# Expert groups in units 4 to 14 instead of 3 to 14, and the diagonal selects of units 1 to 3 split anew between GpSimd and VectorE

## Chip, cores and metric

The kernel runs on one core of a Trainium2 chip. The metric is device microseconds of one execution. A core has five engines with an instruction stream each: TensorE (PE), VectorE (DVE), ScalarE (ACT), GpSimd (POOL) and SyncE (SP, which here only issues transfers). Each stream runs strictly in its own order; semaphores tie the streams together.

## What is computed

A transformer layer without mask padding: x is 4 x 1024 tokens of 128 numbers, all float32. The layer norm xn goes into two branches, whose results are added to x.

```python
def _L0_attn_ref(x, w_qkv, w_proj, b_proj):          # 16 heads of 8, causal
    q, k, v = jnp.split(x @ w_qkv, 3, axis=-1)
    ...
    wei = jnp.einsum('bhqd,bhkd->bhqk', q, k) * scale
    wei = jnp.where(causal, wei, -jnp.inf)
    wei = jax.nn.softmax(wei, axis=-1)
    out = jnp.einsum('bhqk,bhkd->bhqd', wei, v)
    ...
    return out @ w_proj + b_proj

def _L0_ffn_ref(x, Wg, W1, b1, W2, b2):               # 8 experts of 512, the best 2 of each token
    logits = xt @ Wg.T
    topk_logits, topk_idx = jax.lax.top_k(logits, TOP_K)
    w = jax.nn.softmax(topk_logits, axis=-1)
    ...
    h = jax.nn.gelu(jnp.einsum('th,ehi->tei', xt, W1) + b1, approximate=False)
    o = jnp.einsum('tei,eih->teh', h, W2) + b2
    y = jnp.einsum('te,teh->th', gates, o)
x = x + _L0_attn_ref(xn, ...) + _L0_ffn_ref(xn, ...)
```

## The kernel before

**Units and steps.** The attention is cut into 16 units (4 sequences x 4 groups of 4 heads). A unit has ten steps, `SUB`: steps 0 to 2 take the triangle of the first 512 queries (1, 2 and 1 blocks of 128 x 128 on the diagonal), steps 3 to 6 the full square, steps 7 to 9 the triangle of the last 512 queries. "(n, s)" below is unit n, step s. In a step PE makes transposed scores for two pairs of heads ("scores", L919), ACT turns them into `probs` with the exponential (L804), the part above the diagonal is set to zero in the steps of `DIAG`, and PE multiplies with v ("values", L936). The values of step s stand in PE's stream within step s + 1. `probs` has two buffers by step, so the exponentials of step s wait for the values of step s - 2.

**Maxima.** The exact row maxima are found ahead: "max" parts (L899 on PE, L1134 and L1136 on DVE), 36 a unit, are taken from one stream that runs some 27 ahead of the unit. `counts(n)` says how many each step takes.

**The triangles.** Two ways do the same: `SELS`, an affine select on GpSimd (L720), and `CLEARS`, a scalar_tensor_tensor on DVE (L1146) that multiplies with a 0/1 triangle. `scatters_in(n, s)` chooses: DVE where it is true. Before, that is all diagonal steps of units 1 and 2 and steps 0 to 2 of unit 3. PE's values wait for whichever it is.

**Experts.** DVE sorts the tokens by expert while unit 0 runs (the "route" parts). GpSimd then scatters the 32 tiles of normed rows twice (two experts a token) to `xs` in HBM with 64 indirect DMAs (L712), one part "scatter" each, spread over 20 steps from (0, 9) to (2, 8), three or four at the end of each step. A scatter waits for the second last before it to have landed (`UNDER_WAY` = 2). The 39 blocks of 256 sorted rows are done in groups, one group a unit, `FFN_UNIT` = units 3 to 14, three or four blocks each: sizes 3, 3, 3, 4, three times over. SP loads a group's rows ("load_rows", L603), w1 ("load_up", L615), w2 and biases ("load_down", L625 to L630). PE transposes the rows ("rows_in", L977), ACT and DVE split them into a high part (L834) and a low part (L1073), then come "hidden" (12 products a block on PE, L853 to L855, four Gelus on ACT, L816) and "down" (two a block, L997, added to the bias on DVE, L1184), and GpSimd sends the rows back with an indirect DMA ("send", L735).

**The general group** (units 4 to 14): its rows are loaded in step 6 of the unit before and transposed in steps 8 and 9, each before the values of that step's part. All its hidden blocks stand at the start of the unit, ahead of step 0, with three maxima behind each (`BESIDE_M`). The downs stand in steps 1 to 8 or 2 to 7.

**Group 0** (unit 3) is an exception: its rows need all scatters. So they are loaded in (3, 3), transposed in (3, 5) and (3, 6), its hidden blocks stand at the end of (3, 6) and its downs in (3, 7) and (3, 8). SP waits for all scatters at "load_rows" and at the first "reload" (L594, x read again for the residual), both in (3, 3).

**The fill.** `fill` adds "warm" products without use (L949) to a step whose PE work is under `aim(n, s)` columns: 2900 in units of `FFN_UNIT`, 4000 in the others, 3300 in the last.

Of the kernel before, what the change touches and what calls it, by code (L numbers as in the profile page):

```python
# [22 lines left out]
UNITS = B * G4  # L23
# [41 lines left out]
SECOND = 3  # L65
# [6 lines left out]
HALF_M = HG * 3  # L72
EARLY_M = 18

FFN_UNIT = list(range(3, UNITS - 1))
GROUP_OF = {u: f for f, u in enumerate(FFN_UNIT)}
NGRP = len(FFN_UNIT)
FIRST = [NBLK * f // NGRP for f in range(NGRP + 1)]
# [1 line left out]

NORM_TILES = [range(0, 4), range(4, 8)] + [range(TPB * b, TPB * b + TPB) for b in range(1, B)]
PIECES = 13
CLEAR_FROM, CLEAR_UNTIL = (1, 0), (3, SECOND)
SCATTER_FROM, SCATTER_STEPS = 9, 20
UNDER_WAY = 2
VECTOR_NORMS = 3
BESIDE_M = 3
# [3 lines left out]
def scatters_in(n, s):  # L91


    return CLEAR_FROM <= (n, s) < CLEAR_UNTIL


def blocks_of(f):

    return range(FIRST[f], FIRST[f + 1])
# [33 lines left out]
def with_negations(group):  # L133


    return list(group) + [("negate", x[1], int(x[2] == NM - 1)) for x in group if x[2] in (HALF_M - 1, NM - 1)]
# [40 lines left out]
def row_phase(n, s, maxima):  # L177


    low, high = [x for x in maxima if x[2] % HG < 2], [x for x in maxima if x[2] % HG >= 2]  # L180
    first = [(low, 1), (high, 0)] if len(low) >= len(high) else [(high, 0), (low, 1)]
    parts = []
    for beside, half in first:
        parts += beside[:1] + [("scores", n, s, half)] + beside[1:]
    return parts


def counts(n):


    if n in GROUP_OF and GROUP_OF[n] > 0:
        rest = NM - BESIDE_M * len(blocks_of(GROUP_OF[n]))
        return [rest * (i + 1) // NS - rest * i // NS for i in range(NS)]
    first = [9, 9] if n == 0 else [5, 4]
    rest = 0 if n == UNITS - 1 else 27 - (BESIDE_M * len(blocks_of(0)) if n == FFN_UNIT[0] else 0)
    return first + [rest * (i + 1) // 8 - rest * i // 8 for i in range(8)]


def unit_parts(n, stream):

    parts, f, nf = [], GROUP_OF.get(n), GROUP_OF.get(n + 1)
    late_rows = []

    def take(count):
        group = with_negations([next(stream) for _ in range(count)])
        late_rows.extend(("rows",) + x[1:] for x in group if x[0] == "negate")
        return group

    def late_values():
        if n > 0:  # L210
            parts.extend([("values", n - 1, NS - 1), ("evacuate", n - 1, 1)])

    if n >= 1 and n + 2 < UNITS:
        parts.append(("relay", n + 2))
    if f:
        for b in blocks_of(f):
            parts.append(("hidden", f, b))
            if b - FIRST[f] == 1:
                late_values()
            parts.extend(take(BESIDE_M))  # L220
        if f + 1 < NGRP:
            parts.append(("load_up", f + 1))
    subs = [(b, u) for b in blocks_of(f) for u in range(BK // P)] if f is not None else []
    step_of = [7, 7, 7, 8, 8, 8] if f == 0 else list(range(2, 8)) if len(subs) == 6 else list(range(1, 9))
    for s in range(NS):
        due, late_rows[:] = list(late_rows), []
        group = take(counts(n)[s])
        parts.append(("step", n, s))
        only = [x for x in group if x[0] == "max"]
        parts.extend(row_phase(n, s, only[:4]))  # L230
        parts.extend(x for x in group if x not in only[:4])
        if s == 0 and not f:
            late_values()
        if nf and s in (8, 9):
            parts.append(("rows_in", nf, s - 8))
        if s > 0:
            parts.append(("values", n, s - 1))
        parts.extend(due)
        parts.extend(BESIDE.get((n, s), []))
        if s == 1 and n > 0:  # L240
            parts.append(("turn", n - 1, 1))
        parts.extend(("send", f) + x for x, at in zip(subs, step_of) if at == s - 1)
        parts.extend(("down", f) + x for x, at in zip(subs, step_of) if at == s)
        if s == SECOND:
            parts.append(("evacuate", n, 0))
        if s == 3 and n % G4 == 0 and n > 0:
            parts.append(("columns", n // G4 - 1, 1))
        if s == 5:
            parts.append(("turn", n, 0))
        if s in (4, 6) and (n == 6 or (n % G4 == 0 and n > G4)):  # L250
            parts.append(("project", 0 if n == 6 else n // G4 - 1, s // 2 - 2))
        if s in (2, 3, 4, 5) and n % G4 == 1 and n // G4 + 1 < B:
            parts.append(("qk", n // G4 + 1, s % 2, s // 2 - 1))
        if s == 7 and n % G4 == G4 - 1:
            parts.append(("columns", n // G4, 0))
        if s == NS - 1 and n == UNITS - 1:
            parts.append(("project", B - 1, 0))
        if (n, s) in ((2, 3), (2, 7)):
            parts.append(("load_up", 0) if s == 3 else ("load_down", 0))
        if f == 0 and s == 3:  # L260
            parts.append(("load_rows", 0))
        if f == 0 and s in (3, 5, 7, 8):
            parts.append(("reload", (3, 5, 7, 8).index(s)))
        if f == 0 and s in (5, 6):
            parts.append(("rows_in", 0, s - 5))
        if f == 0 and s == 6:
            for b in blocks_of(0):
                parts.append(("hidden", 0, b))
                parts.extend(take(BESIDE_M))
            parts.append(("load_up", 1))  # L270
        if s == (9 if f == 0 else 8) and f is not None and f + 1 < NGRP:
            parts.append(("load_down", f + 1))
        if nf and s == 6:
            parts.append(("load_rows", nf))
        step = NS * n + s - SCATTER_FROM
        if 0 <= step < SCATTER_STEPS:
            parts.extend([("scatter", 0, 0)] * (TOPK * NT * (step + 1) // SCATTER_STEPS - TOPK * NT * step // SCATTER_STEPS))
        if n == UNITS - 1 and s in (0, 2):
            parts.extend(("fetch_back", b) for b in range(B) if (b > 0) == (s > 0))
        if n == UNITS - 1 and s in (2, 4, 6, 8):  # L280
            b = (2, 4, 6, 8).index(s)
            parts.append(("combine", b))
            if b < B - 1:
                parts.append(("store", b, 0))
    parts.extend(late_rows)
    return parts
# [70 lines left out]
EVAC = {x: i for i, x in enumerate(x for x in SCHED if x[0] == "evacuate")}  # L357

SELS = {x: i for i, x in enumerate(x for x in SCHED if x[0] == "scores" and x[2] in DIAG and not scatters_in(*x[1:3]))}
CLEARS = {x: i for i, x in enumerate(x for x in SCHED if x[0] == "scores" and x[2] in DIAG and scatters_in(*x[1:3]))}  # L360
TURNS = {x: i for i, x in enumerate(x for x in SCHED if x[0] == "turn")}
# [878 lines left out]
```

How the kernel before makes its waits and increments, by code:

```python
def wait(eng, sem, value):  # L392
    if value > 0:
        eng.wait_ge(sem, value)
# [136 lines left out]
        @block.sync  # L532
# [9 lines left out]
            sp.dma_start(b2s, b2).then_inc(b_loaded, 16)  # L542
            sp.dma_start(bps, b_proj.partition_broadcast(E)).then_inc(b_loaded, 16)
            experts = {}
            for part in SCHED:
                what = part[0]
                if what == "relay":
                    n = part[1]
                    i, rows = n % 3, slice(32 * (n % G4), 32 * (n % G4) + 32)
                    if n < 3:
                        sp.wait_ge(zeroed, 7)
                    else:
                        sp.wait_ge(sc_ready, both(PAIRI, n - 3, NS - 1))
                    if n % G4 == 0:
                        sp.wait_ge(aux_d, D_AFTER["qk", n // G4, 1, 1])
                    for r in range(3):
                        sp.dma_start(kT[i][r:P:4, :].bitcast(F32), (kqh, kql, kqh)[r][rows, 0, :].bitcast(F32)) \
                            .then_inc(relayed[i], 16)
# [4 lines left out]
                    if n >= 3:  # L564
                        sp.dma_start(qT[i][3:P:4, :].bitcast(F32), mid(zero[0:32, :], T // P)).then_inc(relayed[i], 16)
                elif what == "bias_out":
                    sp.wait_ge(smallT_done, 1)
                    sp.dma_start(b1_scr.rearrange("p e c -> p (e c)"), b1T).then_inc(b_stored, 16)
                    sp.wait_ge(b_summed, 1)
                    sp.dma_start(b2_scr, b2s).then_inc(b_stored, 16)
                elif what == "fetch":
```

## Time and profile before

| | us |
|---|---|
| median of 3 runs | 746.47 |
| the runs | 744.14, 746.47, 948.12 |
| the profiled execution | 744.73 |
| its span, first to last instruction | 742.8 |

Engines busy in the span: PE 659.0 us (89%), DVE 529.3 (71%), ACT 441.5 (59%), POOL 265.0 (36%). The mean granted clock of TensorE is 0.90 of full speed; it moves between 0.5 (1.2 GHz) and 1.0 (2.4 GHz). All times below are microseconds from the start of the span.

The windows further down run between two starts of PE's work. Those of rows 7 go from values product to values product: 163.2 (2, 0), 175.6 (2, 3), 191.6 (2, 8), 199.6 (3, 0), 213.2 (3, 3), 268.4 (4, 0), 277.2 (4, 3), 117.5 (1, 0), 154.6 (1, 8); the last one is a stretch of low clock. Those of rows 8 go from a unit's first hidden product to the next unit's; 255.78 is unit 4's.

### The profile page before, as it was taken

The page shows a single profiled execution, that of the slowest core. Times are in us where ns is not written, and L with a number is a line of the kernel's source. Part 1 is how long each engine was busy: PE and PEld are TensorE (multiplying, and loading weights), DVE is VectorE, ACT ScalarE, POOL GpSimd, SP SyncE. Part 2 cuts the span into 40 slices and gives each one's busy share as a digit, 9 for nine tenths or more (in the row PEclk, how much of TensorE's full clock was granted, in tenths as well). Part 3 has the DMA queues.
Part 4 walks back from the last instruction along what each step waited for, and adds up shares of the span by engine and source line. Part 5 has one row for each costly group of instructions (what it writes and reads, how often), then busy time and mean ns, then how long its engine had stood idle before and what let it go on. Part 6 is the DMA issues. An engine that isn't in the chain of part 4 may idle for free.

```text
span 742.8 us, 14540 instructions
## 1 busy us (share of the span) xinstructions
PE 659.0 (89%) x4867; PEld 385.9 (52%) x4867; DVE 529.3 (71%) x1805; ACT 441.5 (59%) x656; POOL 265.0 (36%) x423
## 2 busy tenths in 40 slices
PE   6899678888866999989999999899999999999986
PEld 5674334344424655545665555546565655555533
DVE  5758887697933576777677676777677776778666
ACT  5223454546434676768576776767576766667654
POOL 5813155655450423231333333231333232333411
PEclk9655796789866999999999999998999999999989
DMA  6651963134514735435251525335252616240075
GB/s 159 199 113 21 238 178 102 47 86 138 126 44 130 221 123 125 138 100 161 80 137 44 154 85 131 130 109 152 82 161 68 172 35 155 94 115 12 26 184 160
DMA packets 99289, 87.93 MB, mean 118 GB/s; under 512 B 13296, under 2 KB 86704, under 8 KB 99216
## 3 DMA queue, kind: packets, MB, share of 16 engines
q1 hardware_dynamic: 94320, 76.69, 38.6%
q0 software_dynamic: 4544, 9.35, 3.7%
q10 hardware_dynamic: 352, 0.97, 0.6%
q8 instruction: 39, 0.64, 0.4%
q14 instruction: 34, 0.28, 0.1%
HBM read 49.79 MB, written 20.80 MB: 95 GB/s over the span
## 4 chain that ended last, share of the span: by engine, by line
PE 63%; DVE 18%; ACT 9%; issue 5%; DMA 3%; ACTq 0%; POOL 0%; SPq 0%; DVEq 0%; POOLq 0%
PE ov L936 17%; PE aux L899 13%; PE aux L997 10%; DVE junk L1136 5%; ACT probs L804 3%; DVE maxes L1134 3%; PE sc L853 3%; PE aux L949 3%; PE aux L954 2%; PE sc L919 2%; PE sc L854 2%; PE sc L855 2%; DVE xrow L1197 2%; ACT hid L816 1%; ACT L804 1%
## 5 line engine op out<-in xcount | busy, mean ns | idle before, releaser
L804 ACT ACTIVATE probs<-sc 128x1024 f32<-128x1024 f32 (+1 forms) x320 | 286.6, 941 | 171.3 <-PE sc L919 156.5
L1136 DVE CUSTOM_DVE_ANT_0 junk<-aux,cst 128x128 bf16<-128x128 f32 (+3 forms) x512 | 220.5, 486 | 33.2 <-PE aux L899 30.1
L899 PE MATMUL aux<-kT,qT 32*128 32x512 f32 (+3 forms) x768 | 200.4, 446 | 34.5 <-DVE maxes L1136 8.1
L1134 DVE TENSOR_REDUCE maxes<-aux 128x1 f32<-128x512 f32 x256 | 163.2, 683 | 38.3 <-PE aux L899 33.5
L720 POOL TENSOR_SCALAR_AFFINE_SELECT probs<-probs 128x256 f32<-128x256 f32 x216 | 85.3, 408 | 275.2 <-ACT probs L804 270.3
L936 PE MATMUL ov<-probs,v 128*32 128x512 f32 (+3 forms) x1536 | 173.5, 542 | 0.7 <-POOL probs L720 0.6
L899 PEld LDWEIGHTS aux<-kT,qT 32*128 32x128 f32 x768 | 90.3, 197 | 123.5 <-DVE maxes L1136 29.9
L919 PE MATMUL sc<-qT,kT 32*128 32x512 f32 (+3 forms) x768 | 142.7, 427 | 5.5 <-DMA qT<-mT 3.2
L735 POOL DMA_INDIRECT ys<-ysb,back x78 | 75.5, 968 | 101.9 <-DVE ysb L1184 55.4
L997 PEld LDWEIGHTS aux<-w2all,hid 128*128 128x128 f32 x624 | 77.6, 196 | 38.2 <-DVE maxes L1134 22.6
L997 PE MATMUL aux<-w2all,hid 128*128 128x128 f32 x624 | 89.3, 288 | 0.3 <-DVE kql L1073 0.3
L712 POOL DMA_INDIRECT xs<-xrow,wall x64 | 62.4, 974 | 50.6 <-DMA xs<-xrow,wall 26.1
L816 ACT ACTIVATE hid<-sc,bias 128x256 f32<-128x256 f32 x156 | 61.2, 476 | 27.4 <-PE sc L855 26.4
L919 PEld LDWEIGHTS sc<-qT,kT 32*128 32x128 f32 x768 | 68.8, 195 | 13.7 <-ACT probs L804 7.5
L936 PEld LDWEIGHTS ov<-probs,v 128*32 128x32 f32 x1536 | 34.9, 113 | 53.1 <-issue 45.3
L1184 DVE TENSOR_TENSOR ysb<-aux,bias 128x128 f32<-128x128 f32 x78 | 22.7, 291 | 48.2 <-PE aux L997 47.3
L949 PE MATMUL aux<-wh 128*128 128x384 f32 x174 | 48.8, 400 | 7.9 <-DVE maxes L1136 4.6
L853 PE MATMUL sc<-xsh,w1b 128*128 128x256 f32 x156 | 48.2, 309 | 0.0
L949 PEld LDWEIGHTS aux<-wh 128*128 128x128 f32 x174 | 32.8, 215 | 24.6 <-DVE maxes L1136 13.0
L854 PE MATMUL sc<-xsl,w1b 128*128 128x256 f32 x156 | 44.1, 283 | 0.0
L855 PE MATMUL sc<-xsh,w1b 128*128 128x256 f32 x156 | 44.0, 282 | 0.0
L1136 DVE DVE_READ_ACCUMULATOR2_ANT maxes<- 128x1 f32 x512 | 42.3, 83 | 0.0
(121 smaller groups left out, 605.3 us busy)
## 6 DMA issues: line engine op xcount, KB each, us to landing
w1b<-w_scr SPq DMA_DIRECT2D x39, 512.0 KB, 4.8
w2all<-in_L_ffn_W SPq DMA_DIRECT2D x39, 256.0 KB
xs<-ysb SPq DMA_DIRECT2D x13, 387.0 KB, 8.1
kT<-kqh SPq DMA_DIRECT2D x32, 128.0 KB
w_scr<-w1b SPq DMA_DIRECT2D x8, 512.0 KB
qT<-kqh SPq DMA_DIRECT2D x30, 128.0 KB
xrow<-in_L_attn_x SPq DMA_DIRECT2D x7, 512.0 KB, 5.8
xsin<-xs SPq DMA_DIRECT2D x9, 387.0 KB
```

Source lines behind the costliest of these rows:

```text
L720: last_ = nc.gpsimd.affine_select(out=block_, in_=block_, compare_op=ALU.is_ge, fill=0.0, base=0, pattern=[[0, 2], [1, P]], channel_multip ...
L735: nc.gpsimd.indirect_dma_start(out=ys[:, :], out_offset=bass.IndirectOffsetOnAxis(ap=back[:, f % 2, i:i + 1], axis=0), in_=ysb[:, i, :], i ...
L804: nc.scalar.activation(probs[:, s % 2, 2 * half:2 * half + 2, 0:cols], pair(part)[:, :, 0:cols], ACT.Exp).then_inc(sc_done, 1)
L816: last_ = nc.scalar.activation(hid[:, i, ch, :], pair(part)[:, ch // 2, BK * (ch % 2):BK * (ch % 2) + BK], ACT.Gelu, bias=bias[i][:, ch:ch ...
L853: nc.tensor.matmul(out_, wh_, mh, start=True, stop=False)
L899: last_ = nc.tensor.matmul(bank(part)[:, at:at + cols], qT[n % 3][rows, P * i:P * i + P], kT[n % 3][rows, k0:k0 + cols], start=True, stop= ...
L919: last_ = nc.tensor.matmul(pair(part)[:, h % 2, at:at + cols], kT[n % 3][rows, P * j:P * j + P], qT[n % 3][rows, q:q + cols], start=True, ...
L936: last_ = nc.tensor.matmul(ov[32 * h:32 * h + 32, W - cols:W], v[:, vat:vat + 32], probs[:, s % 2, h, at:at + cols], start=(j == 0), stop= ...
L949: nc.tensor.matmul(bank(unit)[:, 0:FILL], src[:, 0:P], src[:, 0:FILL], start=True, stop=True)
L997: last_ = nc.tensor.matmul(bank(part)[:, 0:C], hid[:, i, ch, P * u:P * u + P], w2b[i][:, ch, :], start=(ch == 0), stop=(ch == CH - 1))
L1134: last_ = nc.vector.reduce_max(dst, src, axis=AX.X)
L1136: last_ = nc.vector.tensor_tensor_reduce(out=junk[:, AUXI[part] % 3, at:at + cols], in0=src, in1=cmask[:, W - cols:W], scale=1.0, scalar=L ...
```

## The change

- `FFN_UNIT` becomes units 4 to 14, so eleven groups share the 39 blocks: 3, 4, 3, 4, 3, 4, 3, 4, 3, 4, 4. Group 0 (still three blocks) stands in unit 4 in the general form: hidden blocks ahead of step 0, downs in steps 2 to 7.
- What is special about group 0 stays only in its loads: w1 in (3, 3), w2 and biases in (3, 7), where before it was (2, 3) and (2, 7); rows in (3, 8), transposed both at the end of (3, 9), behind the values there. The reloads of x move from unit 3 to unit 4.
- Unit 3 has no expert work. Its aim is then 4000 columns a step, and its maxima are spread as in unit 2.
- `scatters_in` is true only for steps from 3 on, and up to the end of unit 3: the steps 7 to 9 of units 1 to 3 are cleared on DVE, the steps 0 to 2 of units 1 to 3 are selected on GpSimd. There they stand in GpSimd's stream between the scatters, each at the place of its step.
- The scatters keep their places.

```diff
--- before.py
+++ after.py
@@ -72,7 +72,7 @@
 HALF_M = HG * 3
 EARLY_M = 18
 
-FFN_UNIT = list(range(3, UNITS - 1))
+FFN_UNIT = list(range(4, UNITS - 1))
 GROUP_OF = {u: f for f, u in enumerate(FFN_UNIT)}
 NGRP = len(FFN_UNIT)
 FIRST = [NBLK * f // NGRP for f in range(NGRP + 1)]
@@ -80,7 +80,7 @@
 
 NORM_TILES = [range(0, 4), range(4, 8)] + [range(TPB * b, TPB * b + TPB) for b in range(1, B)]
 PIECES = 13
-CLEAR_FROM, CLEAR_UNTIL = (1, 0), (3, SECOND)
+CLEAR_FROM, CLEAR_UNTIL = (1, 0), (4, 0)
 SCATTER_FROM, SCATTER_STEPS = 9, 20
 UNDER_WAY = 2
 VECTOR_NORMS = 3
@@ -91,7 +91,7 @@
 def scatters_in(n, s):
 
 
-    return CLEAR_FROM <= (n, s) < CLEAR_UNTIL
+    return CLEAR_FROM <= (n, s) < CLEAR_UNTIL and s >= SECOND
 
 
 def blocks_of(f):
@@ -188,11 +188,11 @@
 def counts(n):
 
 
-    if n in GROUP_OF and GROUP_OF[n] > 0:
+    if n in GROUP_OF:
         rest = NM - BESIDE_M * len(blocks_of(GROUP_OF[n]))
         return [rest * (i + 1) // NS - rest * i // NS for i in range(NS)]
     first = [9, 9] if n == 0 else [5, 4]
-    rest = 0 if n == UNITS - 1 else 27 - (BESIDE_M * len(blocks_of(0)) if n == FFN_UNIT[0] else 0)
+    rest = 0 if n == UNITS - 1 else 27
     return first + [rest * (i + 1) // 8 - rest * i // 8 for i in range(8)]
 
 
@@ -212,7 +212,7 @@
 
     if n >= 1 and n + 2 < UNITS:
         parts.append(("relay", n + 2))
-    if f:
+    if f is not None:
         for b in blocks_of(f):
             parts.append(("hidden", f, b))
             if b - FIRST[f] == 1:
@@ -221,7 +221,7 @@
         if f + 1 < NGRP:
             parts.append(("load_up", f + 1))
     subs = [(b, u) for b in blocks_of(f) for u in range(BK // P)] if f is not None else []
-    step_of = [7, 7, 7, 8, 8, 8] if f == 0 else list(range(2, 8)) if len(subs) == 6 else list(range(1, 9))
+    step_of = list(range(2, 8)) if len(subs) == 6 else list(range(1, 9))
     for s in range(NS):
         due, late_rows[:] = list(late_rows), []
         group = take(counts(n)[s])
@@ -229,7 +229,7 @@
         only = [x for x in group if x[0] == "max"]
         parts.extend(row_phase(n, s, only[:4]))
         parts.extend(x for x in group if x not in only[:4])
-        if s == 0 and not f:
+        if s == 0 and f is None:
             late_values()
         if nf and s in (8, 9):
             parts.append(("rows_in", nf, s - 8))
@@ -255,23 +255,18 @@
             parts.append(("columns", n // G4, 0))
         if s == NS - 1 and n == UNITS - 1:
             parts.append(("project", B - 1, 0))
-        if (n, s) in ((2, 3), (2, 7)):
+        if nf == 0 and s in (3, 7):
             parts.append(("load_up", 0) if s == 3 else ("load_down", 0))
-        if f == 0 and s == 3:
+        if nf == 0 and s == 8:
             parts.append(("load_rows", 0))
         if f == 0 and s in (3, 5, 7, 8):
             parts.append(("reload", (3, 5, 7, 8).index(s)))
-        if f == 0 and s in (5, 6):
-            parts.append(("rows_in", 0, s - 5))
-        if f == 0 and s == 6:
-            for b in blocks_of(0):
-                parts.append(("hidden", 0, b))
-                parts.extend(take(BESIDE_M))
-            parts.append(("load_up", 1))
-        if s == (9 if f == 0 else 8) and f is not None and f + 1 < NGRP:
+        if s == 8 and f is not None and f + 1 < NGRP:
             parts.append(("load_down", f + 1))
         if nf and s == 6:
             parts.append(("load_rows", nf))
+        if nf == 0 and s == 9:
+            parts.extend(("rows_in", 0, i) for i in range(2))
         step = NS * n + s - SCATTER_FROM
         if 0 <= step < SCATTER_STEPS:
             parts.extend([("scatter", 0, 0)] * (TOPK * NT * (step + 1) // SCATTER_STEPS - TOPK * NT * step // SCATTER_STEPS))
```

## Rows read from the trace of the kernel before

**Rows 1.** Page, part 4: the chain that ended last, by engine.
```profile
PE 63%; DVE 18%; ACT 9%; issue 5%; DMA 3%; ACTq 0%; POOL 0%; SPq 0%; DVEq 0%; POOLq 0%
```

**Rows 2.** Timeline of PE (start us, us; in brackets the idle time before, and its releaser).
```profile
229.71 1.08 PE L977 MATMUL aux<-cst,xsin 128*128 128x128 f32 x4 [12.27 <-DMA xsin<-xs]
```

**Rows 3.** Timeline of GpSimd from 117 to 224: eight of the 64 scatters.
```profile
117.13 0.96 POOL L712 DMA_INDIRECT xs<-xrow,wall  x1 [0.30 <-issue]
...
169.50 0.96 POOL L712 DMA_INDIRECT xs<-xrow,wall  x1 [0.81 <-issue]
...
177.73 0.95 POOL L712 DMA_INDIRECT xs<-xrow,wall  x1 [2.59 <-DMA xs<-xrow,wall]
180.22 0.96 POOL L712 DMA_INDIRECT xs<-xrow,wall  x1 [1.53 <-DMA xs<-xrow,wall]
...
187.63 0.96 POOL L712 DMA_INDIRECT xs<-xrow,wall  x1 [1.92 <-DMA xs<-xrow,wall]
189.69 0.96 POOL L712 DMA_INDIRECT xs<-xrow,wall  x1 [1.10 <-DMA xs<-xrow,wall]
193.44 0.96 POOL L712 DMA_INDIRECT xs<-xrow,wall  x1 [2.79 <-DMA xs<-xrow,wall]
...
223.87 0.95 POOL L712 DMA_INDIRECT xs<-xrow,wall  x1 [0.78 <-DMA xs<-xrow,wall]
```

**Rows 4.** Timeline of PE: the first values products of (2, 2) and (3, 0).
```profile
172.48 0.64 PE L936 MATMUL ov<-probs,v 128*32 128x256 f32 x8
...
199.65 1.94 PE L936 MATMUL ov<-probs,v 128*32 128x512 f32 x8
```

**Rows 5.** Groups by line and form: busy us, mean ns; then idle before.
```profile
L720 POOL TENSOR_SCALAR_AFFINE_SELECT probs<-probs 128x256 f32<-128x256 f32 x216 | 85.3, 408 | 275.2 <-ACT probs L804 270.3 <-DVE maxes L1134 1.2 <-issue 0.3
...
L1146 DVE SCALAR_TENSOR_TENSOR probs<-probs,cst 128x256 f32<-128x256 f32 x40 | 16.1, 422 | 2.8 <-ACT probs L804 1.7 <-issue 1.0
...
L1073 DVE TENSOR_TENSOR xsl<-aux,xsh 128x512 fp32r<-128x512 f32 x15 | 10.4, 691 | 22.5 <-ACT xsh L834 22.5
...
L834 ACT CAST xsh<-aux 128x512 fp32r<-128x512 f32 x15 | 8.9, 593 | 13.6 <-PE aux L977 13.2
```

**Rows 6.** Timeline of SP's queue: w1 and w2 of group 0, its rows.
```profile
171.63 2.75 SPq L615 DMA_DIRECT2D w1b<-w_scr  x3
...
183.43 0.45 SPq L625 DMA_DIRECT2D w2all<-in_L_ffn_W  x1
...
226.21 0.39 SPq L603 DMA_DIRECT2D xsin<-xs  x1
```

**Rows 7.** Windows: length, busy PE PEld DVE ACT POOL, clock, DMA share, GB/s.
```profile
163.20:175.60 12.40, 11.21 (x82) 5.94 (x84) 9.85 (x43) 5.23 (x9) 6.96 (x8) 0.83 0.35 104
175.60:191.60 16.00, 13.98 (x103) 5.90 (x102) 13.73 (x39) 10.13 (x13) 6.94 (x7) 1.00 0.53 146
199.60:213.20 13.60, 12.47 (x65) 5.72 (x64) 7.48 (x32) 4.63 (x8) 8.17 (x9) 0.50 0.14 46
268.40:277.20 8.80, 8.30 (x85) 4.78 (x80) 5.87 (x25) 5.94 (x9) 3.80 (x8) 1.00 0.06 18
117.50:154.60 37.10, 32.51 (x181) 15.05 (x180) 26.63 (x86) 17.66 (x24) 22.79 (x24) 0.74 0.14 46
...
222.00:235.70 13.70, 5.99 (x29) 3.80 (x30) 2.49 (x10) 3.74 (x5) 2.10 (x3) 0.50 0.45 120
```

**Rows 8.** Windows from first hidden product to the next unit's: units 4, 10 to 13.
```profile
255.78:294.26 38.48, 36.20 (x305) 21.20 (x301) 28.68 (x99) 28.26 (x43) 15.57 (x28) 1.00 0.48 132
...
502.69:545.49 42.80, 41.36 (x329) 26.17 (x325) 29.59 (x101) 28.73 (x45) 12.66 (x23) 0.92 0.37 108
545.49:582.99 37.50, 35.74 (x306) 21.01 (x302) 28.28 (x99) 27.51 (x42) 13.66 (x26) 1.00 0.45 123
582.99:623.37 40.38, 37.62 (x322) 22.81 (x318) 29.52 (x101) 27.59 (x42) 12.25 (x23) 1.00 0.40 110
623.37:662.18 38.81, 36.98 (x304) 21.30 (x300) 28.38 (x99) 27.13 (x41) 12.25 (x23) 0.96 0.46 131
```

## The prediction

> **What bounds the kernel now.** I read the page first: the chain that ended last runs through PE for 63% of the span, DVE 18%, ACT 9%, GpSimd (POOL) 0% [rows 1]. So a stretch costs what PE has to do in it, and GpSimd's work costs nothing. The longest idle times of PE show the exception: once it waits 12.27 us, up to 229.71, for the load of the expert rows [rows 2]. GpSimd's and SP's timelines give the chain behind it: the last of 64 scatters starts on GpSimd at 223.87, SP issues the load of group 0's rows at 226.21, PE goes on 3.5 us later [rows 3, 6]. The transposes that wait stand in unit 3, step 5, and need every scatter; the written order ends the scatters in step 8 of unit 2, whose values start at 191.6 [rows 7]. They run 32 us behind it. The reason is that only two may be under way: a pair is issued 0.3 us apart, 0.96 each, then GpSimd waits 0.8 for a landing [rows 3], which makes 3.0 us a pair at best and more, up to 2.8 us a gap, where SP's transfers run.
>
> **Now GpSimd's order matters.** Before, units 1 and 2 ask nothing of GpSimd but scatters; DVE clears the triangles. After, the selects of steps 0 to 2 stand in GpSimd's queue behind the scatters of the steps before: three before (1,0) (unit, step), 35 before (2,0), 38 before (2,1), 41 before (2,2), and all 64 before (3,0). They are late by what is queued ahead of them. Behind a select waits the values product of its step, and behind that all of PE's stream.
>
> **What the selects cost.** One costs 408 ns on GpSimd, the clear on DVE 422 ns [rows 5]. Steps 0 to 2 have eight (1+2+1 blocks, two halves), so 24 move to GpSimd, and 8 (unit 3, steps 7 to 9) go to DVE. DVE gains 16 x 0.42 = 6.8 us net. I price that at nothing: where it falls PE will wait for GpSimd, or it works at half clock with DVE idle beside it, as in unit 3 before (PE busy 12.5 of 13.6 us, DVE 7.5 [rows 7]). If that cover were gone it would be worth the whole 6.8.
>
> The Trainium skill, page GPSIMD Engine Reference, § 4.1, speaks against the move: elementwise work belongs on VectorE, GpSimd being about twice as slow with two inputs and about equal with one. The two rows above have equal durations, the select having one input tensor; with twice the price the sum below would be about 7 us higher (an estimate).
>
> **Unit 1.** The fourth scatter starts at 117.13 after 0.30 idle, so the third ends at 116.83 [rows 3]; the two selects of (1,0) then end near 117.7, and the values product before started at 117.5 [rows 7]. The next two steps shift PE by 0.5 to 1 us and the scatters by about 1.2, since part of the 3.3 us of selects lies in the waits for a landing. No more.
>
> **Unit 2.** The 35th scatter started at 169.50 [rows 3]; with that shift it ends near 171.7. Its select follows, and values (2,0) start near 172.7 instead of 163.2 [rows 7]. Three scatters (two at 1.3, one at 1.9 with its wait) and four selects later it is (2,1) at about 178.4, then (2,2) at 183.5, before 172.48 [rows 4]. PE is 11 us late. It needs no select until (3,0): before, (2,2) to (3,0) took 199.65 - 172.48 = 27.2 us [rows 4], so it arrives at 210.7, some us later if its clock has fallen in the waits.
>
> **The last scatter.** Before it ended at 224.8 [rows 3]. Added: 1.2 (unit 1) and 2.0 (unit 2: 3.3 us of selects less what lies in landings). Removed: group 0's w1 and w2 loads, issued at 171.63 and 183.43 [rows 6], leave unit 2 for unit 3. Near them the gaps were 2.59 and 1.53, then 1.92 and 1.10, where an ordinary pair has 0.8 + 0.4 [rows 3]; that gives back 2.9 + 1.8. The relay of unit 5 that runs near 193 stays, and with it a gap of 2.79 and another like it. Sum: 224.8 + 3.2 - 4.7 = 223.3. Bounds: 219.4 if the relay's excess of 2 x 2 us goes as well, 231.4 if nothing is given back and all 16 selects count in full. Two selects on top: values (3,0) start at 224.2 instead of 199.65. PE waits up to 13 us there. The old wait of 12.3 us has moved, it is not gone.
>
> **Unit 3 from there.** No expert work, but filled up to 4000 columns a step and with the same maxima as unit 2, so unit 2 is the model. Its steps 0 to 3 took 12.4 us, at a mean clock of 0.83; unit 3's own took 13.6 at 0.50, unit 4's 8.8 at 1.00. After the wait the clock will be at its low level for a while, as it was from 222.0 to 235.7 [rows 7]. I take 12.4, bounds 8.8 and 13.6: (3,3) at 236.6. Steps 3 to 8 of unit 2 took 16.0 [rows 7]: (3,8) at 252.6, and its product takes 1.0. Now comes what other groups don't have: group 0's rows are loaded in step 8 and transposed in step 9, directly before the first hidden product. SP issues nine transfers (w2 and biases) ahead of that load; in unit 2 they began 8 us before (2,8). Alone, the load took under 3.5 us from issue [rows 2, 6]. I take 1 us of waiting (0 to 3). The load's own wait for the scatters is long over by step 8. Then four transposes (1.08 at the low clock [rows 2], I take 0.8), the cast 0.6 and the subtraction 0.7 [rows 5] are in sequence: 2.1. First hidden product of unit 4: 253.6 + 1.0 + 2.1 = 256.7, before 255.8 [rows 8]: +0.9 us. The four reloads of x go with group 0 into unit 4; the first reader is the projection in unit 6, so they cost nothing.
>
> **Units 4 to 15.** At that point the kernel before has group 0's three blocks behind it, the kernel after has not. Eleven groups follow in both, with 36 blocks before and 39 after. From first hidden product to first hidden product it took 42.8 us with four blocks (unit 10) and 37.5, 40.4 and 38.8 with three (units 11, 12, 13; 12 also projects) [rows 8]. PE is busy 41.4 and 37.0 of it in units 10 and 13: the block is PE work, and no cover hides it. I take unit 13, which like 10 has neither projection nor columns: 4.0 us a block, bounds 2.4 (against 12) and 5.3 (against 11). Three blocks: +12.0 us (7.2 to 15.9). What a group costs beside its blocks comes eleven times in both. The transfers of a fourth block are hidden: the DMA share in unit 10 is 0.37 [rows 8].
>
> **Sum.** 0.9 + 12.0 = +12.9 us on a span of 742.8: 755.7. The profiled execution took 744.7 in all, so 757.6. The median of the three runs, 746.5, is 1.8 above it; 757.6 is 1.5% above the median.
>
> **The rivals.**
> - *The queue holds PE, and the clock stays low behind it: slower by over 2%.* Place: unit 3, steps 0 to 8. Unit 1 took 37.1 us for them at a mean clock of 0.74 and with its qk products, unit 2 took 12.4 + 16.0 = 28.4 [rows 7]. If unit 3 costs as unit 1, +8.7: 766. It decides from +3.8 on, which is 761.4. For it: in unit 3 before the clock was low with PE busy. Against it: after the old wait it was back 6 us after PE went on [rows 2, 7]. Chance 0.18. A dearer block (5.3), or a scatter stream without relief, leads over the same line (761.5 and more): 0.18 together.
> - *The queue doesn't hold PE.* If GpSimd came to (3,0) by 210.7, all falls by 13.5: 744, no change. It would need 1.1 us a scatter from (2,2) on, below the 0.96 + 0.30 of two issues in a row [rows 3]. Chance 0.05.
> - *DVE was the bound in units 1 to 3.* Its 6.8 us count in full, with the low ends for block and steps: 757.6 - 6.8 - 4.8 - 3.6 = 742. DVE is busy 13.7 of 16.0 us in the second half of unit 2 [rows 7], but there nothing is taken from it. Chance 0.06. Below 731.5 comes only this together with the one above: 0.05.
> - *The forecast,* 746 to 761: 0.48.
>
> About 2% is what a measurement of this kernel can tell from no change, so faster means under 731.5 and slower over 761.4. Chances: faster 0.05, within 2% 0.48 + 0.05 + 0.06 = 0.59, slower 0.36. The low ends together (3.9 + 3.6 + 1.0 + 4.8) give 744.3, the high ends (8.1 + 1.2 + 2.0 + 3.9) 772.8; eight in ten lie in 746 to 769.
>
> **What would show each step.** Right: PE idle in front of values (2,0) and again some 10 us in front of (3,0), each wait ended by a GpSimd select; the last scatter at 219 to 227; no 12 us wait for the rows; first hidden product of unit 4 within 250 to 262; 499 us from there to the end instead of 487. Wrong: values (3,0) before 215; four blocks in a cycle under 41 us; scatters at 1.5 us each all through unit 2; the clock low through most of unit 3.

## The result, and the profile after

The changed kernel takes 758.5 us (median of four runs, 758.0 to 762.1). Beside it the kernel before took 745.3, a median over four runs with the 948.12 among them, which the ratios leave out like every other run in the chip's slower state. The ratio is 1.0191, 95% interval 1.0145 to 1.0238: clearly slower, but the 2% that was set to separate "no change" from "slower" lies inside the interval. The profiled execution took 758.3, its span is 756.2, against 755.7 forecast. The line numbers of the functions are five smaller than before (L931 is the values product that was L936).

The page's chain that ended last, by engine, to set beside [rows 1]:

```profile
PE 57%; DVE 16%; issue 12%; ACT 6%; DMA 5%; SPq 2%; POOL 1%; ACTq 0%; POOLq 0%; DVEq 0%
```

GpSimd itself is still nearly absent. But the page's split of this chain by line now has `DMA xs<-xrow,wall`, the landings of the scatters, with 3%. "issue" (time for which the profile shows no cause) went from 5% to 12%. In the list of waits (engine and line, releaser: us in total, times, the longest) one line has grown. Before it stood at 0.6 us, once:

```profile
PE ov L931 <- POOL probs L715: 27.4, 6, 11.0
```

PE's timeline (start us, us; idle before and its releaser) shows the two long ones, at values (2,0) and (3,0). Three of the other four are 1.83 us at (1,0), 2.09 at (1,1) and 1.53 at (2,1).

```profile
162.92 0.50 PE L894 MATMUL aux<-kT,qT 32*128 32x512 f32 x1
174.44 1.08 PE L931 MATMUL ov<-probs,v 128*32 128x512 f32 x4 [11.02 <-POOL probs L715]
...
213.42 0.79 PE L894 MATMUL aux<-kT,qT 32*128 32x512 f32 x1
224.64 1.88 PE L931 MATMUL ov<-probs,v 128*32 128x512 f32 x5 [10.43 <-POOL probs L715]
```

GpSimd's timeline at the same places shows why. The exponentials of (2,0) ended at 160.8 and those of (3,0) at 211.0; the selects came only when the 35th and the 64th scatter had been issued, nearly 13 us later, and both scatters had waited for landings:

```profile
172.56 0.96 POOL L707 DMA_INDIRECT xs<-xrow,wall  x1 [0.81 <-DMA xs<-xrow,wall]
173.53 0.77 POOL L715 TENSOR_SCALAR_AFFINE_SELECT probs<-probs 128x256 f32<-128x256 f32 x2
...
222.75 0.96 POOL L707 DMA_INDIRECT xs<-xrow,wall  x1 [0.81 <-DMA xs<-xrow,wall]
223.73 2.19 POOL L715 TENSOR_SCALAR_AFFINE_SELECT probs<-probs 128x256 f32<-128x256 f32 x6
```

The last row holds six selects in a stretch without a gap: two of (3,0) and four of (3,1) had been ready. The wait of [rows 2] is gone: group 0's rows now hold PE for 0.38 us, and the sequence of transposes, cast and subtraction for another 1.07:

```profile
252.99 1.94 PE L931 MATMUL ov<-probs,v 128*32 128x384 f32 x16
255.30 1.51 PE L972 MATMUL aux<-cst,xsin 128*128 128x128 f32 x6 [0.38 <-DMA xsin<-xs]
257.88 0.55 PE L848 MATMUL sc<-xsh,w1b 128*128 128x256 f32 x1 [1.07 <-DVE xsl L1068]
```

SP's queue, to set beside [rows 6]: the loads of w1 and w2 of group 0 are past the last scatter, the rows' load comes 5.8 us behind the first w2.

```profile
232.69 2.62 SPq L610 DMA_DIRECT2D w1b<-w_scr  x3
...
244.45 0.45 SPq L620 DMA_DIRECT2D w2all<-in_L_ffn_W  x1
...
250.20 0.39 SPq L598 DMA_DIRECT2D xsin<-xs  x1
```

Windows with the columns of [rows 7]: unit 3 from (3,0) to (3,3) and on to (3,8), then everything from unit 4's first hidden product to the end:

```profile
224.60:236.60 12.00, 10.98 (x81) 5.82 (x83) 6.09 (x29) 4.66 (x8) 2.13 (x6) 0.84 0.23 67
236.60:253.00 16.40, 14.07 (x102) 5.84 (x102) 14.13 (x39) 10.67 (x14) 0.00 (x0) 0.98 0.39 118
257.90:756.20 498.30, 467.11 (x3763) 282.84 (x3763) 354.71 (x1203) 334.18 (x501) 152.73 (x280) 0.97 0.43 119
```

The kernel before, from its first hidden product of unit 4 on, had three blocks less in the same eleven groups:

```profile
255.78:742.80 487.02, 452.31 (x3677) 268.54 (x3673) 351.22 (x1197) 329.66 (x490) 150.23 (x279) 0.97 0.41 114
```

So the 13.4 us of span split into +2.1 up to that product (257.9 against 255.8) and +11.3 behind it. The stretch before (3,0) is no fixed length either: three more profiles below (36 blocks, and rows early twice) are of kernels with the same instructions up to there. In the four of them PE reached the wait between 214.2 and 216.3 and left it between 223.8 and 225.2; the wait was 10.4, 9.7, 8.6 and 8.0 us. What PE loses before it, the wait gives back.

### The profile page after: what moved, and what is told of

Same layout as the page of the kernel before. It is cut to its first block, busy times and chain, and to the rows that moved or that the text cites. A ratio compares the mean times of both kernels' runs of the same rounds, so it can differ in the third digit from the quotient of the medians.

```text
span 756.2 us, 14558 instructions
## 1 busy us (share of the span) xinstructions
PE 660.9 (87%) x4884; PEld 390.1 (52%) x4884; DVE 524.9 (69%) x1787; ACT 438.8 (58%) x652; POOL 270.1 (36%) x438
## 4 chain that ended last, share of the span: by engine, by line
PE 57%; DVE 16%; issue 12%; ACT 6%; DMA 5%; SPq 2%; POOL 1%; ACTq 0%; POOLq 0%; DVEq 0%
PE ov L931 14%; PE aux L894 12%; PE aux L992 10%; DVE junk L1131 6%; PE sc L848 3%; ACT probs L799 3%; PE aux L944 3%; DMA xs<-xrow,wall 3%; PE aux L949 2%; PE sc L849 2%; PE sc L850 2%; PE sc L914 2%; DVE xrow L1192 2%; DVE maxes L1129 2%; PE aux L972 1%
## 5 line engine op out<-in xcount | busy, mean ns | idle before, releaser
L1131 DVE CUSTOM_DVE_ANT_0 junk<-aux,cst 128x512 bf16<-128x512 f32 (+3 forms) x512 | 219.6, 487 | 33.7 <-PE aux L894 28.5
L931 PE MATMUL ov<-probs,v 128*32 128x512 f32 (+3 forms) x1536 | 172.1, 538 | 27.7 <-POOL probs L715 27.4
L715 POOL TENSOR_SCALAR_AFFINE_SELECT probs<-probs 128x256 f32<-128x256 f32 x232 | 91.3, 408 | 280.1 <-ACT probs L799 274.6
L914 PE MATMUL sc<-qT,kT 32*128 32x512 f32 (+3 forms) x768 | 140.0, 423 | 5.6 <-DMA qT<-mT 3.3
L931 PEld LDWEIGHTS ov<-probs,v 128*32 128x32 f32 x1536 | 35.2, 113 | 80.9 <-issue 68.6
L944 PE MATMUL aux<-wh 128*128 128x384 f32 x191 | 52.3, 395 | 8.9 <-DVE maxes L1131 6.2
L944 PEld LDWEIGHTS aux<-wh 128*128 128x128 f32 x191 | 35.4, 212 | 26.4 <-DVE maxes L1131 15.3
```

The source lines that it names most:

```text
L715: last_ = nc.gpsimd.affine_select(out=block_, in_=block_, compare_op=ALU.is_ge, fill=0.0, base=0, pattern=[[0, 2], [1, P]], channel_multip ...
L914: last_ = nc.tensor.matmul(pair(part)[:, h % 2, at:at + cols], kT[n % 3][rows, P * j:P * j + P], qT[n % 3][rows, q:q + cols], start=True, ...
L931: last_ = nc.tensor.matmul(ov[32 * h:32 * h + 32, W - cols:W], v[:, vat:vat + 32], probs[:, s % 2, h, at:at + cols], start=(j == 0), stop= ...
L944: nc.tensor.matmul(bank(unit)[:, 0:FILL], src[:, 0:P], src[:, 0:FILL], start=True, stop=True)
L1131: last_ = nc.vector.tensor_tensor_reduce(out=junk[:, AUXI[part] % 3, at:at + cols], in0=src, in1=cmask[:, W - cols:W], scale=1.0, scalar=L ...
```

## The experiments

The theory: PE pays for selects that stand behind scatters in GpSimd's order; the scatters are slow because each second one waits for a landing; and three more blocks cost PE about 4 us each. "H" is the start of unit 4's first hidden product, "tail" the span from there to the end. Ratios are to the kernel before on the same chip. Kernels 3, 4, 5 and 8 of the table ran on one chip, 7, 9 and 10 on a second, 6 on a third. The ratio of one and the same program has differed by 2.4% between two chips (last experiment), more than the intervals say, so ratios of different chips are compared with that in mind. The starts in the profiles carry the argument.

| kernel | us | ratio, 95% interval | last scatter issued | H | tail |
|---|---|---|---|---|---|
| before | 745.3 | | 223.9 | 255.8 | 487.0 |
| changed | 758.5 | 1.019 (1.015 to 1.024) | 222.8 | 257.9 | 498.3 |
| groups alone | 736.9 | 0.985 (0.979 to 0.992) | 228.7 | 237.4 | 498.6 |
| selects alone | 759.5 | 1.018 (1.013 to 1.024) | 227.3 | 270.0 | 486.9 |
| changed, unit 3 on DVE | 756.6 | 1.015 (1.010 to 1.020) | 221.4 | 251.0 | 501.6 |
| groups, unit 1 alone on GpSimd | 736.6 | 0.982 (0.974 to 0.991) | 226.8 | 239.5 | 493.5 |
| changed, 36 blocks | 751.0 | 1.009 (1.005 to 1.012) | 223.4 | 259.8 | 489.4 |
| changed, four under way | 739.0 | 0.990 (0.985 to 0.994) | 199.1 | 234.6 | 499.8 |
| groups alone, four under way | 732.2 | 0.983 (0.975 to 0.991) | 203.2 | 234.7 | 495.6 |
| **before, four under way** | **728.4** | **0.979 (0.971 to 0.987)** | 202.1 | 242.2 | 484.6 |

### The two parts of the change, each alone

Groups alone, on the changed kernel:

```diff
-    return CLEAR_FROM <= (n, s) < CLEAR_UNTIL and s >= SECOND
+    return CLEAR_FROM <= (n, s) < CLEAR_UNTIL
```

> The groups part of the change alone: eleven groups in units 4 to 14, but all diagonal steps of units 1 to 3 cleared on DVE, so GpSimd's queue holds nothing but scatters there. Queue theory (PE pays for selects queued behind scatters): no PE wait before values (2,0) and (3,0); values (3,0) near 200; first hidden product of unit 4 near 233 (225 to 236) instead of 257.9; time 733 (728 to 740), faster than before. Rival (the three blocks more and unit 3's filled steps cost it all, and the wait at (3,0) only stands where another would be): 755 to 759. Rival (rows of group 0 are late again, the scatters not having ended in time): a PE wait of 5 us or more before the transposes in (3,9), 738 or more.

736.9 us, faster than before. There is no long wait at (2,0) or (3,0), and (3,0) starts at 198.7. H is 4 us later than the 233 forecast, though, and the second rival is right about the wait, if not about the time (738 or more): the rows were late.

```profile
227.64 1.27 PE L931 MATMUL ov<-probs,v 128*32 128x384 f32 x16
234.82 1.51 PE L972 MATMUL aux<-cst,xsin 128*128 128x128 f32 x6 [5.90 <-DMA xsin<-xs]
```

The reason is in GpSimd's and SP's rows. PE reaches unit 3 before the scatters are over, so the loads of w1 and w2, now in unit 3, run beside them again:

```profile
224.41 1.12 POOL L707 DMA_INDIRECT xs<-xrow,wall  x1 [1.58 <-ACT probs L799]
228.66 1.20 POOL L707 DMA_INDIRECT xs<-xrow,wall  x1 [3.12 <-DMA xs<-xrow,wall]
...
207.65 2.77 SPq L610 DMA_DIRECT2D w1b<-w_scr  x3
...
219.41 0.45 SPq L620 DMA_DIRECT2D w2all<-in_L_ffn_W  x1
```

From first to last issue the scatters took 117.2 us without a single select among them, 113.5 in the kernel before, 111.0 in the changed kernel with 16 selects among them. The loads make the difference. The next kernel, selects alone, has the same 16 selects in the stream as the changed one, but the loads of group 0 beside it, and takes 117.1. In the changed kernel PE stands still until the scatters are through, and so the loads come behind them.

Selects alone, on the kernel before:

```diff
-CLEAR_FROM, CLEAR_UNTIL = (1, 0), (3, SECOND)
+CLEAR_FROM, CLEAR_UNTIL = (1, 0), (4, 0)
...
-    return CLEAR_FROM <= (n, s) < CLEAR_UNTIL
+    return CLEAR_FROM <= (n, s) < CLEAR_UNTIL and s >= SECOND
```

> The selects part alone: groups as before (units 3 to 14), but steps 0 to 2 of units 1 to 3 selected on GpSimd and steps 7 to 9 of units 1 to 3 cleared on DVE. Queue theory: values (2,0) start near 173 and values (3,0) near 229, since the loads of group 0 still run beside the scatters; the old wait of 12.3 us for the rows disappears; first hidden product of unit 4 near 271 against 255.8 before; time 760 (755 to 766). Rival (the selects are neutral, one wait takes the other's place): 745 to 748.

759.5 us, H 270.0, as forecast (760, 271). PE's wait at (3,0) is the longest of all variants, since here the loads still slow the scatters:

```profile
229.16 1.88 PE L936 MATMUL ov<-probs,v 128*32 128x512 f32 x5 [14.24 <-POOL probs L720]
```

So the change is made of a part that gains 1.5% and one that loses 1.8% alone; together they lose 1.9%. The two don't add. In H the parts are 18.4 us earlier and 14.2 us later alone, and 2.1 us later together. One reason lies in the rows above: group 0's rows need the last scatter in any case. Groups in unit 4 can hide that wait, but not behind a PE that has itself waited for the scatter.

### Which selects

```diff
-    ... < CLEAR_UNTIL and s >= SECOND
+    ... < CLEAR_UNTIL and (s >= SECOND or n == 3)
```

> The changed kernel with steps 0 to 2 of unit 3 alone back on DVE; units 1 and 2 as changed. Queue theory: the wait of 11 us at values (2,0) stays, the one of 10.4 at (3,0) goes; values (3,0) near 213, first hidden product of unit 4 near 246, time 747 (743 to 751). Rival (the wait at (3,0) is paid anyway, at the rows of group 0): time 756 to 759 with a PE wait of 8 us or more before the transposes in (3,9).

756.6 us: the forecast of 747 is missed, and the time is the rival's (756 to 759), but its reason is wrong too. It asked for a wait of 8 us or more at the rows, and PE waits 1.5 us there:

```profile
248.41 1.51 PE L972 MATMUL aux<-cst,xsin 128*128 128x128 f32 x6 [1.49 <-DMA xsin<-xs]
```

H came down by 6.9 us instead of 12. Two windows from (2,2) to the arrival at (3,0), first this kernel, then the changed one up to the start of its wait:

```profile
185.90:216.70 30.80, 26.97 (x182) 12.01 (x181) 23.69 (x78) 17.01 (x21) 18.03 (x19) 0.83 0.26 72
```

```profile
186.40:214.20 27.80, 23.85 (x179) 11.01 (x177) 23.32 (x76) 17.24 (x21) 15.52 (x17) 0.95 0.29 75
```

The instructions are nearly the same (two clears of (3,0) more on DVE), and the granted clock was 0.83 against 0.95 after the same wait at (2,0). In the changed kernel such a loss vanishes in the wait at (3,0), as the four profiles above show; here it counts. The rest of the miss is the tail, 501.6 at a clock of 0.96 (below), and a median 2.2 us above the profiled execution. A wait that is cut out can return less than its length, as it had covered other losses.

```diff
+    ... < CLEAR_UNTIL and (s >= SECOND or n > 1)
```

> The groups in units 4 to 14, two scatters under way, selects on GpSimd only in steps 0 to 2 of unit 1; units 2 and 3 on DVE. Queue theory: in unit 1 only three, six and nine scatters stand ahead, so PE loses at most 1.5 us there and the time is that of the groups alone, 737 (733 to 741). Rival (any select between scatters holds PE): 743 or more.

736.6 us, the time of the groups alone, as forecast. But the selects are not harmless even with three, six and nine scatters ahead. They hold PE for 4.9 us in three waits, not for 1.5 at most, and (3,0) starts at 204.3 instead of 198.7. At the rows the wait is shorter in return, 1.1 us instead of the 5.9 of the groups alone:

```profile
PE ov L931 <- POOL probs L715: 4.9, 3, 2.7
...
236.96 1.51 PE L972 MATMUL aux<-cst,xsin 128*128 128x128 f32 x6 [1.11 <-DMA xsin<-xs]
```

What is left is H 2.1 us later, and a tail that happened to be 5.1 us shorter (0.98 against 0.97 of clock) covers that. So the equal times are in part luck. The waits of 10 us and more still need the 35 and 64 scatters.

### The length of the scatter stream

```diff
-UNDER_WAY = 2
+UNDER_WAY = 4
```

> The changed kernel with four scatters under way instead of two. If GpSimd waits for landings (theory), a scatter costs about 1.27 us and the queue keeps up with PE: last scatter near 200, waits at (2,0) and (3,0) under 3 us each, time 735 (730 to 742). Rival (the scatters are bound by GpSimd's own work or by the DMA engines): 1.5 us or more a scatter, last scatter after 215, time 752 to 759.

739.0 us on the changed kernel, 2.9% less by the two ratios, through one number. Now scatters in a row run at the issue rate of GpSimd, 1.27 us each; over the whole stream, with 16 selects in it, it is 1.41. Ahead of (2,0) and at the end of the stream:

```profile
158.35 0.95 POOL L707 DMA_INDIRECT xs<-xrow,wall  x1 [0.30 <-issue]
159.62 0.96 POOL L707 DMA_INDIRECT xs<-xrow,wall  x1 [0.30 <-DMA xs<-xrow,wall]
160.59 0.77 POOL L715 TENSOR_SCALAR_AFFINE_SELECT probs<-probs 128x256 f32<-128x256 f32 x2
...
199.06 0.96 POOL L707 DMA_INDIRECT xs<-xrow,wall  x1 [0.30 <-issue]
200.03 2.19 POOL L715 TENSOR_SCALAR_AFFINE_SELECT probs<-probs 128x256 f32<-128x256 f32 x6
```

What is left of the waits in its list is a third of the 27.4 us of the changed kernel:

```profile
PE ov L931 <- POOL probs L715: 8.5, 3, 4.8
```

The same number in the kernel before:

> The kernel before with four scatters under way instead of two, nothing else. Theory (the whole case is the length of the scatter stream): last scatter near 200, no PE wait for group 0's rows in (3, 5), first hidden product of unit 4 near 242 instead of 255.8, time 731 (725 to 736). Rival (the rows' wait was paid for something else too, or DMA traffic makes up for it): 739 or more.

728.4 us, H 242.2: both as forecast, and the lowest time of all. The transposes of group 0's rows no longer wait:

```profile
216.60 0.66 PE L954 MATMUL aux<-cst,ot 128*128 128x128 f32 x4
217.09 0.60 PE L977 MATMUL aux<-cst,xsin 128*128 128x128 f32 x4
```

And with the groups moved, but all triangles on DVE:

> Groups in units 4 to 14, all triangles of units 1 to 3 cleared on DVE, four scatters under way. Against the changed kernel with four under way (739.0) only the place of 24 selects differs. Queue theory: the rest of the waits at (2,0) and (3,0), some 3 and 2 us, goes too; first hidden product of unit 4 near 231, time 734 (729 to 739). Rival (DVE was a bound in units 1 to 3 and its relief is worth the 6.8 us): 743 or more.

732.2 us; H is 234.7, the same as with 24 selects on GpSimd (234.6). That is not because nothing differed on the way. With the selects on GpSimd PE waits 4.8 us at (2,0) and 3.2 at (3,0), but it is ahead before them: steps 0 to 3 of unit 1 take 13.2 us instead of 15.2. First the selects on GpSimd, then the clears on DVE:

```profile
116.30:129.50 13.20, 10.50 (x74) 5.00 (x73) 9.09 (x38) 6.91 (x11) 10.83 (x15) 0.88 0.17 54
```

```profile
118.20:133.40 15.20, 13.01 (x76) 6.26 (x75) 11.16 (x46) 6.93 (x11) 8.39 (x10) 0.70 0.13 42
```

DVE is busy 2.1 us less and the granted clock is 0.88 against 0.70; which of the two saves the time is not separated. From values (1,0) to (1,8) it is 33.1 us against 37.1. A further 1.9 us stand already at (1,0), before the first select.

The two kernels ran on different chips, so their 739.0 and 732.2 don't compare better than their ratios do. Moving the groups gained 1.5% with two under way. With four it gained nothing: 732.2 with it and 728.4 without, on one chip. It was a remedy for the late scatters, paid with three blocks in units that are full, and with the cause gone there is nothing to buy.

### The blocks

```diff
-FIRST = [NBLK * f // NGRP for f in range(NGRP + 1)]
+FIRST = [(NBLK - 3) * f // NGRP for f in range(NGRP + 1)]
```

> The changed kernel with 36 blocks in the eleven groups instead of 39; the last three blocks (rows of the last experts) are left out, so this part of the output is missing. Block theory (a block costs PE 4 us wherever it stands): 12 us less from unit 4's first hidden product to the end, 486 to 488 instead of 498.3 to 501.6; time 746.5 (743 to 750). Rival (blocks are partly hidden, and the price is in the grouping): 3 to 6 us less, 753 or more.

751.0 us, tail 489.4, that is 9 us less than the changed kernel's instead of the 12 expected. Tails of the same instructions differ, though, and go with the mean granted clock. With 39 blocks, unit 1 alone on GpSimd and then unit 3 on DVE:

```profile
239.50:733.00 493.50, 462.19 (x3763) 278.89 (x3763) 354.96 (x1203) 334.27 (x501) 152.95 (x280) 0.98 0.43 121
```

```profile
251.00:752.60 501.60, 468.93 (x3763) 284.87 (x3763) 354.96 (x1203) 334.12 (x501) 154.97 (x280) 0.96 0.42 119
```

and with 36 blocks, before with four under way:

```profile
242.20:726.80 484.60, 449.99 (x3677) 267.60 (x3673) 351.14 (x1197) 328.90 (x489) 149.87 (x278) 0.98 0.41 115
```

All tails by their clock, but for the one with the pauses of the last experiment (493.2 with 36 blocks at 0.97):

| mean clock of the tail | 39 blocks | 36 blocks |
|---|---|---|
| 0.98 | 493.5, 495.0 | 484.6 |
| 0.97 | 495.6, 498.3, 498.6 | 486.9, 487.0, 489.0, 489.4 |
| 0.96 | 499.8, 501.6 | |
| 0.95 | 506.8 | |

The clocks are rounded to hundredths. At equal clock the means differ by 9.7 and 9.4 us, some 3.2 us a block. The 11.3 between the profiles of the two kernels come from one tail of its group's upper end (498.3) and one of its lower end (487.0). The stretches of low clock fall in different units from execution to execution.

Nor does a block cost the same everywhere. From first hidden product to first hidden product, all at a clock of 1.00, unit 9 and unit 11 with three blocks (before):

```profile
460.32:502.69 42.37, 38.48 (x316) 22.58 (x312) 30.77 (x103) 29.47 (x45) 12.25 (x23) 1.00 0.43 125
545.49:582.99 37.50, 35.74 (x306) 21.01 (x302) 28.28 (x99) 27.51 (x42) 13.66 (x26) 1.00 0.45 123
```

and with four (unit 1 alone on GpSimd):

```profile
447.58:492.00 44.42, 42.20 (x342) 26.12 (x338) 31.99 (x105) 31.00 (x49) 13.25 (x25) 1.00 0.37 104
529.29:570.34 41.05, 39.39 (x334) 24.68 (x330) 29.55 (x101) 29.25 (x46) 13.32 (x25) 1.00 0.40 112
```

In both units the fourth block adds 3.7 us of PE work. It costs 3.6 us in unit 11, where PE was idle for 1.8 us of the stretch, and 2.0 in unit 9, where it was idle for 3.9. (In unit 9 the next group, whose rows are transposed there, has one block less in the second kernel. In unit 8 one block more in the next group made 0.2 us.)

### Rows early

```diff
-        if nf and s in (8, 9):
+        if nf is not None and s in (8, 9):
             parts.append(("rows_in", nf, s - 8))
...
-        if nf == 0 and s == 8:
-            parts.append(("load_rows", 0))
...
-        if nf and s == 6:
+        if nf is not None and s == 6:
             parts.append(("load_rows", nf))
-        if nf == 0 and s == 9:
-            parts.extend(("rows_in", 0, i) for i in range(2))
```

> The changed kernel with group 0's rows loaded in (3,6) and transposed in (3,8) and (3,9) ahead of the values, as for every other group. From the start of values (3,8) to the first hidden product it took 4.9 us in the changed kernel; forecast: 2 to 2.5 (the values product and nothing else), first hidden product of unit 4 near 255.5, the time 2 us or so less, below what one run can tell. Rival (the gap is not due to the late rows): 4.5 to 5.

> The changed kernel with group 0's rows loaded in (3,6) and transposed in (3,8) and (3,9), timed. The one look gave 765.4, with the first hidden product of unit 4 at 256.7 and 507 us from there to the end instead of 498. Forecast from the place that was edited: 756 (753 to 760). If the tail of 507 belongs to this program: 763 or more.

At the place that was edited it did what was expected; hidden follows values without a gap:

```profile
254.19 1.94 PE L927 MATMUL ov<-probs,v 128*32 128x384 f32 x16
256.05 0.58 PE L844 MATMUL sc<-xsh,w1b 128*128 128x256 f32 x1
```

H is 256.1 instead of 257.9. The first time it ran, a single execution, it took 765.4 us, and four runs on another chip took 751.4 (ratio 1.010, 1.002 to 1.019), which misses the forecast of 756 (753 to 760) on the low side. The 14 us between them, and the 7 to 758.5, are more than this edit can do. H was 256.7 and 256.1, but the tails were 506.8 at a mean clock of 0.95 and 495.0 at 0.98, each in line with the table of tails. So the difference goes with the granted clock and not with the edit.

### A program that differed by the chip

> The kernel before with four scatters under way and, in units 1 to 3, steps 0 to 2 selected on GpSimd instead of cleared on DVE (24 clears less). Only this differs from the kernel before with four under way (728.4). Queue theory with a short queue: PE waits 2 to 4 us at values (2,0) and (3,0), little or nothing is gained from DVE; time 728 to 733. Rival (DVE's relief of 10 us counts once the queue is short): 718 to 723.

Its edit is that of the selects alone, with `CLEAR_UNTIL` at (3, 0) and four under way. It took 756.7 us (ten runs, 751.8 to 758.2; ratio 1.012, 1.007 to 1.016), far over the forecast. No wait on GpSimd explains it: PE waits for a select once, for 2.7 us, and values (3,0) start at 221.1, 3 us behind selects that were done. But three times all of PE, DVE and ACT stood still together, for 3.5, 2.3 and 1.9 us. DVE's timeline at one of them:

```profile
140.80 0.19 DVE L1087 SCALAR_TENSOR_TENSOR mneg<-mrow,mneg 128x16 fp32r<-128x16 f32 x1
145.75 0.26 DVE L1160 RECIPROCAL rden<-aux 128x16 f32<-128x16 f32 x1 [4.75 <-remote]
```

> The kernel before with four scatters under way and steps 0 to 2 of units 1 to 3 selected on GpSimd, once more, on whatever chip it falls. The first time it took 756.7 instead of the 728 to 733 forecast, with three pauses of 2 to 3.5 us of PE, DVE and ACT together and a low clock through most of unit 2. If that belongs to the program: 750 or more and the pauses at the same steps. If it belongs to that chip or hour: 728 to 735 and no pause.

On another chip the same program took 735.4 us (ten runs, 733.7 to 737.6; ratio 0.988, 0.985 to 0.991), and the three pauses are absent. So they belong to the chip or the hour. They are 7.7 of the 14.7 us by which H differs (261.5 and 246.8); in the rest the granted clock was lower, 0.73 against 0.84 from (1,0) to (2,0) and 0.70 against 0.78 from there to (3,0). Nor was everything slow on the first chip: unit 1 alone on GpSimd ran there too and took 736.6. And the kernel before took 748.9 there and 746.5 on the other, so the ratio to it did not take the chip out: 1.012 and 0.988 for one program, outside each other's intervals.

The forecast of 728 to 733 is missed by 2 us even so, but its mechanism holds. PE waits 3.8 us at (2,0) and 2.8 at (3,0), where 2 to 4 were expected, and 10.4 us in four waits in all. H is 4.6 us later than without selects on GpSimd (242.2), less than the waits: here too unit 1 is shorter, 32.9 us against 36.3 from (1,0) to (1,8). Even a short queue costs more than it gives.

## Why the prediction was right

The forecast was 757.6 us, 1.5% above the kernel before, with eight in ten for 746 to 769; measured were 758.5 and 1.9%. The likeliest single outcome of the prediction was "within 2%" (0.59), and the measured interval lies on both sides of that line. Point by point, forecast and measured:

| | forecast | measured |
|---|---|---|
| values (2,0) | 172.7 | 174.4 |
| values (2,2) | 183.5 | 186.4 |
| last scatter ends | 223.3 | 223.7 |
| values (3,0) | 224.2 | 224.6 |
| (3,3) | 236.6 | 236.6 |
| (3,8) | 252.6 | 253.0 |
| its product, rows, first hidden product | 4.1 | 4.9 |
| first hidden product of unit 4 | 256.7 | 257.9 |
| from there to the end | 499.0 | 498.3 |
| span | 755.7 | 756.2 |

**The mechanism** was right: the order within GpSimd's queue, not GpSimd's speed, holds PE, at the two places named, and the old wait moved there. The parts alone, the selects of single units and the four scatters under way each change what is queued or how fast it drains, and the waits follow.

**Unit 1** was right by two errors. PE waited 3.9 us at (1,0) and (1,1), where 0.5 to 1 us of shift and "no more" were forecast, yet (1,8) came only 1.4 us later than before (156.0 against 154.6). Something gave most of the wait back; DVE's relief or the clock are the candidates, as with four under way.

**Unit 2** came 1.7 to 2.9 us later than forecast. Of it 1.4 is older than the change: the first scatter started at 111.76 instead of 110.39, in a stretch where both kernels have the same program. The relief by the moved loads was under-sized by about as much: from the 35th to the last scatter it took 50.2 us instead of 54.4 before. With the 2.0 net that the prediction counts for the selects in between, that is 6.2 of relief, where 4.7 had been counted. The two errors cancel in the last scatter, and that is luck. Once (3,0) hangs on the last scatter, everything that PE lost before it is forgiven.

**Unit 3** on the model of unit 2 held within half a microsecond. The product at (3,8) took 1.9 us at the low clock instead of 1.0; the wait for the rows was 0.4 instead of 1.0, the sequence behind it 2.6 instead of 2.1.

**The blocks.** 11.3 us for three was forecast as 12.0, but the price of 4.0 was partly clock. Units 10 and 13 were granted 0.92 and 0.96 [rows 8]; at equal clock the tails give some 3.2 a block, 3.6 in unit 11 and 2.0 in unit 9, so "no cover hides it" holds for some units only. Three blocks are then 9.4 to 9.7 us. That the sum fits to 0.7 us is luck: the profiled execution of the changed kernel has a long tail for its clock, and that of the kernel before a short one.

**DVE's relief** at nothing was right for the changed kernel as a net value, since the waits at (2,0) and (3,0) cover all that comes before. It is not shown that the relief is worth nothing by itself: with four under way, unit 1 is 3.4 to 4.0 us shorter with the selects on GpSimd, and the clock is higher there too. On the price of the select, the Trainium skill, GPSIMD Engine Reference, § 4.1, has GpSimd about equal to VectorE with one input, and the trace fits that: 408 ns for the select again, against 422 for the clear [rows 5]. The clear has two inputs and the select one, so the rows don't test the page's factor of two. The move lost for another reason, the order in the queue.

**The rivals.** "The queue doesn't hold PE" is out: PE waited 10.4 us at (3,0), with GpSimd there at 223.7 and not by 210.7. "DVE was the bound", with a gain of the full 6.8 us in this change, is out as well. The chance of 0.05 for "faster" needed both of these at once and was too high beside 0.05 and 0.06 for each. The clock rival did not come to pass in unit 3 (0.84, then 0.98), but the clock is what blurs the tail.

## What to carry to other kernels

An engine with 36% of busy time can still be the wrong place for a short operation: count what is queued ahead of it at the moment when it is needed, with the waits of those instructions, here some 1.8 us for each scatter. Before moving work away from a late producer, look at what makes it late; one number (four transfers under way instead of two) gave at least as much (2.1%) as the best rearrangement around it (1.5% and 1.8%). A wait that is removed returns less than its length when it has been covering slower stretches ahead of it. And equal totals don't show that nothing changed: compare the starts along the way, as waits of 8 us and a shorter unit 1 came out at the same H.

## What the runs showed of the hardware

- Scatters of 128 rows from GpSimd: with four under way 1.27 us each in a row and 1.41 to 1.46 over the stream of 64 (1.60 in the run with the pauses), with two under way 1.5 at best (a pair in 3.0) and 1.75 to 1.86 over the stream; the issue itself is 0.96 in both. With two under way, gaps of 1.5 to 3 us stand where SP's loads run. With the same 16 selects in it, the stream took 117.1 us with the loads of group 0 beside it (selects alone) and 111.0 without (the changed kernel).
- One program took 756.7 us on one chip and 735.4 on another, ten runs each and neither spread wider than 7 us, with pauses of 1.9 to 3.5 us of three engines together on the first. What pauses them stays open. The ratio to the kernel before on the same chip moved with it, from 1.012 to 0.988, so a difference of 2 to 3% between kernels that ran on different chips says little, even as a ratio.
- The same tail of 3763 matmuls took 493.5 to 501.6 us at mean clocks of 0.98 to 0.96; with the rows early, 506.8 at 0.95.
